# Width-one attention: norms of batches four and five formed in batch zero, and the rounding of batch six begun sooner

## The reference

```python
x = x + _L1_xattn_ref(_layernorm(x, axis=-1), ctx_1024, ctx_1024, ...)
x = x + _L1_ffn_ref(_layernorm(x, axis=-1), L1_ffn_kernel, L1_ffn_input_scale, L1_ffn_kernel_scale, L1_ffn_bias)
x = x + _L2_attn_ref(_layernorm(x, axis=-1), L2_attn_w_qkv, L2_attn_w_out)
```

## Time and profile before

| | |
|---|---|
| median of the runs | 3169.73 us |
| profiled execution | 3159.46 us, span 3157.3 us |
| mean granted clock of the tensor engine | 0.969 |
| tensor engine (PE) busy | 2945.8 us, 93% |
| weight loads (PEld) busy | 1958.1 us, 62% |
| vector engine (DVE) busy | 1865.7 us, 59% |
| ScalarE (ACT) busy | 1253.1 us, 40% |
| GpSimd (POOL) busy | 427.3 us, 14% |

### The profile page before, as it was taken

How to read it: one execution, slowest core, us unless ns; L and a number is a source line. 1 busy time by engine, 2 the same in 40 slices (tenths; PEclk the granted TensorE clock), 3 DMA queues, 4 the chain that set the end, 5 groups by cost and what they waited for, 6 DMA issues and landing times.

```text
span 3157.3 us, 52296 instructions
## 1 busy us (share of the span) xinstructions
PE 2945.8 (93%) x20677; PEld 1958.1 (62%) x20677; DVE 1865.7 (59%) x6449; ACT 1253.1 (40%) x1946; POOL 427.3 (14%) x458
## 2 busy tenths in 40 slices
PE   7999999998989889988998999899999999998998
PEld 4666666875555556655665556566667766766653
DVE  5443433599999636775677888574244344434455
ACT  1222221335656433323443678554322333323443
POOL 0010010114434221000000256300000000000000
PEclk9999999988999989999999899899999999998999
DMA  3000000010000100000000011100000000000000
GB/s 129 1 1 0 1 1 1 1 53 1 2 1 2 34 32 1 1 1 6 2 2 1 23 41 28 41 1 27 1 1 0 1 0 1 1 0 9 2 1 27
DMA packets 22028, 37.75 MB, mean 12 GB/s; under 512 B 2132, under 2 KB 19733, under 8 KB 20760
## 3 DMA queue, kind: packets, MB, share of 16 engines
q1 hardware_dynamic: 20968, 34.02, 3.2%
q10 hardware_dynamic: 816, 0.39, 0.1%
HBM read 26.81 MB, written 2.10 MB: 9 GB/s over the span
## 4 chain that ended last, share of the span: by engine, by line
PE 75%; DVE 17%; ACT 4%; issue 2%; ACTq 0%; DMA 0%; DVEq 0%; SPq 0%; POOL 0%; POOLq 0%
PE ps L416 44%; DVE arena L569 3%; PE ps L621 2%; PE ps L689 2%; PE ps L3093 2%; PE ps L3112 2%; ACT arena L675 2%; PE ps L1628 2%; PE ps L517 2%; DVE arena L1962 2%; PE ps L2348 1%; PE ps L730 1%; PE ps L2394 1%; PE ps L554 1%; PE ps L2966 1%
## 5 line engine op out<-in xcount | busy, mean ns | idle before, releaser
L416 PE MATMUL ps<-weights,arena 128*128 128x256 f32 (+4 forms) x2480 | 695.8, 430 | 40.0 <-DVE arena L1843 22.5
L416 PEld LDWEIGHTS ps<-weights,arena 128*128 128x128 f32 (+1 forms) x2480 | 460.4, 195 | 209.9 <-issue 93.1
L416 PE MATMUL ps<-arena,weights 128*128 128x256 f32 (+4 forms) x1726 | 563.9, 475 | 13.9 <-DMA weights<-in_w_L_attn 6.0
L416 PEld LDWEIGHTS ps<-arena,weights 128*128 128x128 f32 (+1 forms) x1726 | 318.9, 193 | 218.9 <-issue 156.6
L416 PE MATMUL ps<-arena 128*128 128x256 f32 (+4 forms) x1618 | 425.8, 416 | 6.0 <-ACT arena L4811 1.5
L416 PEld LDWEIGHTS ps<-arena 128*128 128x128 f32 (+2 forms) x1618 | 297.9, 188 | 114.7 <-issue 74.7
L569 DVE TENSOR_REDUCE arena<-ps 128x16 f32<-128x1232 f32 (+2 forms) x96 | 179.1, 1865 | 151.1 <-PE ps L547 50.2
L675 ACT ACTIVATE arena<-ps 77x2048 f32<-77x2048 f32 (+1 forms) x112 | 210.0, 1875 | 124.3 <-PE ps L621 62.6
L1962 DVE MATCH_REPLACE8 arena<-arena 128x77 f32<-128x77 f32 x1024 | 214.5, 227 | 0.0
L864 POOL TENSOR_TENSOR x<-x,weights 128x512 f32<-128x512 f32 x32 | 43.8, 1370 | 1196.6 <-DVE arena L830 1148.2
L2361 ACT ACTIVATE arena<-ps 128x1536 f32<-128x1536 f32 x128 | 185.5, 1451 | 49.7 <-PE ps L2350 42.7
(11 more groups left out here) (430 smaller groups left out, 4476.9 us busy)
## 6 DMA issues: line engine op xcount, KB each, us to landing
arena<-arena SPq DMA_DIRECT2D x156, 32.0 KB
weights<-in_w_L_ffn SPq DMA_DIRECT2D x1, 3848.0 KB, 11.5
weights<-in_w_L_attn SPq DMA_DIRECT2D x1, 3840.0 KB, 15.0
weights<-in_w_L_xattn SPq DMA_DIRECT2D x3, 1024.0 KB, 6.3
weights<-in_w_L_ffn SPq DMA_DIRECT2D x1, 3072.0 KB, 10.2
x<-in_x SPq DMA_DIRECT2D x2, 1024.0 KB
weights<-in_w_L_xattn SPq DMA_DIRECT2D x1, 2048.0 KB, 7.4
out<-x SPq DMA_DIRECT2D x8, 256.0 KB, 2.2
```

The source lines that it names most:

```text
L416: ins = k.nc.tensor.matmul(out, lhsT, rhs, start=start and i == 0, stop=i == n - 1)
```

## The change

Two of the places in the vector engine's stream are moved; what is computed stays the same.

```diff
-ROUND_SIX = {(1, 4): (0,), (1, 6): (1,), (1, 8): (2, 3)}
+ROUND_SIX = {(1, 1): (0, 1), (1, 4): (2,), (1, 6): (3,)}
...
-            if at == (1, 1):
+            if at == (0, 6):
                 norms_part_vector(k, dve, s.norms, 1)
...
-            if at == (1, 9):
+            if at == (1, 8):
                 round_last_vector(k, over_six.link, f.power, f.near, flat(f.q)).then_inc(*x.sig.up("f_q"))
                 over_six.close()
```

## The result

The changed kernel takes 3151.96 us, median of six launches (3144.56 to 3155.49), against 3169.66 us for the kernel before (3163.64 to 3172.96) on the same chip: ratio 0.995, 95% interval 0.9938 to 0.9962. The forecast was 3167.5 us, which is 2.3 us of gain; by these medians it is 17.7. The profiled execution took 3144.56 us, with a span of 3142.5.

A forecast was written before the change was run, and what follows sets the result against it. Tensor engine bounds the kernel, so only its pauses cost: + 0.80 − 0.75 − 0.24 − 0.29 − 1.79 = −2.27 us takes the profiled 3159.46 to 3157.2; with the runs' 10.3 us gap, 3167.5 us, range 3164.7 to 3170.3.

The forecast's parts named there:

- What bounds the kernel, and the pauses: Whole kernel: tensor engine busy 2945.8 of 3157.3 us, so only its pauses, or work that makes one, cost time.
- The four pauses of the earlier trace: Tensor engine in batch one, ended by vector instructions: 0.75 (z), 0.24 (queries' copy), 0.29 (mask), 1.84 us (means).
- The norms' price, 2.56 us, new pause 0.80: Norms moved to 1777.80 take 2.56 us, delay batch two's z; tensor engine pauses 0.80 us behind group nine, batch zero.
- The rounding's share, 1.84 to 0.05: Batch one, before the means' transposition (line 2652): with less vector work ahead, the 1.84 us pause shrinks to about 0.05.
- The sum, −2.27 us: Width-one stage: new pause less the old ones, + 0.80 − 0.75 − 0.24 − 0.29 − 1.79 = −2.27 us.
- the rival of the clock: Behind group nine of batch zero: new pause brings the clock down, 8.0 us lost, 3175.5 us; chance 0.03.
- I take the difference as the same for both kernels: Whole time: runs' median 3169.73 lies 10.3 us above the profiled execution; the same gap was added to the changed kernel.
- The late pauses: Rival, batch one: late pauses don't hang on vector load; only 1.28 us come back, −0.5 us, 3169.3; chance 0.15.
- The clock moves further on: Rival, behind 1824: half-clock stretches grow or shrink, ± 3 us, so 3164.5 to 3170.5; chance 0.14.
- Nothing happens: Rival: norms fit the idle time before group seven and later vector load matters as little; 3169.7 us; chance 0.04.

The follow-up runs named there:

- e10: Kernel before with only the norms moved, to group 15 of batch 1, rounding where it was; mean 3156.0 us (3145.7 to 3166.3).
- e3: Kernel before with only the norms moved, to group 6 of batch 0 as in the changed kernel; mean 3154.0 us, ratio 0.9974.
- e6: Kernel before, letter for letter, timed again on the second chip; its profiled execution took 3173.8 us.
- e1: Kernel before, letter for letter, timed beside itself; 3148.2 to 3166.7 us in 12 launches, ratio 0.9997.
- e2: Changed kernel, letter for letter, timed beside the kernel before; 3144.7 to 3156.1 us, ratio 0.9962.
- e8: Changed kernel, letter for letter, second copy, on the second chip; mean 3150.8 us (3144.3 to 3156.6), ratio 0.9979.
- e11: Kernel before, order untouched, with three useless matmuls in its 1.84 us pause for line 2652 in batch 1; mean 3154.9 us, ratio 0.9971.
- e5: Changed kernel with the norms moved to group 15 of batch 1; mean 3146.6 us (3141.1 to 3152.7), ratio 0.9958 to before.
- e9: e7 with four useless matmuls in its pause for line 2652 in batch 1; mean 3146.9 us (3144.5 to 3149.5).
- e7: e5 with rounding step 3 and the two last rounding instructions in group 11 of batch 1; mean 3164.1 us, ratio 1.0024 to before.
- e4: Kernel before with only the rounding moved as in the changed kernel, norms where they stood; mean 3155.5 us, ratio 0.998.

## Why the prediction was wrong

*What bounds the kernel, and the pauses.* Right for the piece. The four pauses of the earlier trace rows were the ones that mattered, and all four went.

*The norms' price, 2.56 us, new pause 0.80.* Mis-sized: 3.17 us and 1.08. I had read that GpSimd is idle from 1777.80 to 1780.15, and then put 2.56 us of work from 1777.80 on, which reaches past it. The collision is in the trace: the instruction at 1769.04 takes 0.62 us, where the same line took 0.16 before, and ends at 1769.66, when the select of 1769.01 does. The first half of z waits 0.18 us more for its result. Against that, z's last half took 0.40 us and not 0.72, so my sum with these two durations gives 0.80 + 0.61 − 0.32 = 1.09. The rule of the Trainium skill ("SBUF — State Buffer", a port pair locked for a whole instruction) agrees with that ending, though it acted at another place than the one where I had let it act: z's halves took 0.42 and 0.40.

*The rounding's share, 1.84 to 0.05.* Right: no pause is shown, and with the norms moved and the rounding not (e10, e3) 0.94 and 0.96 us stay.

*The sum, −2.27 us.* Right for the piece, −2.08. As the change of the whole time it was too small by 7.7 us in the mean, and by 15.4 in the medians of the first comparison.

*The step that failed* has two ends. The first is the rival of the clock, with its chance of 0.03: "the pause of 1.84 us, longer than both ends of my bound, stands in a stretch whose clock is 1.00". One execution showed a pause without a fall, and I took it as what such a pause does. It was one draw: the wait for the same line in e6, 1.97 us long, cost 16.6 us by the fall behind it. I had priced such a fall only for the pause that is added (8.0 us; 6.2 measured) and never asked what the removed one had been costing. The second end is the sentence "I take the difference as the same for both kernels" on the 10.3 us between the profiled 3159.46 us and the median of 3169.73. That gap was the evidence: the launches timed held something that the profile didn't show. Their three times, 3169.6 to 3169.8, lie in the upper group.

*The account by means.* 135 launches of before have a mean of 3160.9 us, 30 of the changed kernel 3150.9, so the change is worth 10.0 us or 0.3%; the 17.7 us of the first comparison are six launches of before that all fell in its upper group. Since that group's share differs by chip, the comparisons side by side are the surer ones: 8.6 us on the chip of e1 and e2, 7.8 us on that of e6 and e8. Of the 10.0, the shorter pauses are 2.1. Two thirds of the launches (88 of 135) had lain 14.9 us above the others, which is 9.7 us in the mean, and no launch of the changed kernel is above 3156.6. The difference is 1.8 us the other way, and the fall that its own new pause brings, at 6.2 us each, has that sign. But it would take such a fall in three launches of ten, and two of the three traces of the changed kernel have one: the account closes to some 2 us and no better. The last two terms are worked out from the groups and not seen launch by launch: of before's upper group I have one trace, which doesn't show how many of its launches owe their place to the fall behind line 2652. That the upper group thins to 3 of 12 when only that wait is filled (e11) speaks for most of them.

*The other rivals.* The late pauses did not stay. "The clock moves further on" was half a thought in the right direction, but about places behind the stage, and with ± 3 us. "Nothing happens" was wrong.

*Still open:* why the wait for the same line is followed by a fall in one launch and not in another; why the clock stays down 13.7 us in batch 0 and 34 to 38 us behind line 2652; and what leads to the falls in batch 4.

## What to carry to other kernels

Where the tensor engine is nearly always busy at full clock, price a pause not by its length but by the length plus the chance of a fall times its cost, and look for the chance in the spread of the timed launches and their clocks; one trace can't give it. A profile that lies apart from the timed launches is a sign that it shows another case than they do. The best kernel here is the one that has no pause left in batches 0 and 1 behind the stage's start (e5, 13 us under the launches of before beside it and 4 under the changed kernel on the same chip). Where a wait can't be moved, a few matmuls of no use in it did as well (e9).

## What the hardware did that I had not expected

- A pause of 1.97 us at full clock (e6) was followed by 37.6 us at half clock, in which 270 matmuls ran, and one of 2.52 us (e7) by 34.2 us. In two other launches of the kernel before (its first trace and e1), the pause for the same line was 1.84 us, and no fall followed.
- Pauses of 1.08 us behind group 9 of batch 0 were followed by 13.7 us at half clock in three of four traces (e2, e3 and e8, but not in the first of the changed kernel), and one of 1.04 us in e4 too, with 0.88 us of waiting shortly ahead of it. Pauses of 0.94 and 0.96 us for line 2652 (e10, e3) and of 0.74 to 0.76 us for line 2573 (the three traces of before, and e11) were followed by none. So length alone doesn't sort them: 1.04 us had a fall behind it, and 1.84 us had none.
- Filling a wait of 2.52 us (e7) with 3.5 us of matmuls (e9) shortened the kernel by 17 us in the mean.
- Up to the first moved instruction, traces of one and the same program differ by up to 11.8 us (1754.07 in e4 against 1765.89 in the first trace of before, for the exponential of group 4 of batch 0). The three traces of the kernel before alone differ by 6.4 us there (1759.49 in e6, 1762.72 in e1). Their falls are at other places.
